# Eight-step graph diffusion, graph convolution with LSTM windows, batch-normed graph layer and edge attention in one kernel: another order of the convolution's steps, norm groups of one batch at the start of attention, and four outputs behind the gates

## The chip, the cores and the metric

One core of one Trainium2 chip runs the whole program. The metric is the device time of one execution in microseconds (us). Engines: PE (TensorE, matrix products), DVE (VectorE), ACT (ScalarE), POOL (GpSimd), SP (SyncE, which only issues DMAs here). Each engine runs its own instructions in the order in which they were written; semaphores hold it where it needs another engine's result.

## What is computed

`x` has 16 batches of 512 nodes with 128 features, `adj` is 512x512. Four graph layers follow each other, each with a residual and a layer norm behind it:

```python
def _layernorm(x, axis=-1, eps=1e-05):
    m = jnp.mean(x, axis=axis, keepdims=True)
    v = jnp.var(x, axis=axis, keepdims=True)
    return (x - m) / jnp.sqrt(v + eps)

# L0: eight Euler steps on h = x @ fc_in_w.T + b
ax = jnp.einsum('nm,bmd->bnd', adj_mx, h)
f = alph * 0.5 * (ax - h) + h @ w_eff - h + x0
h = h + dt * f
# L1: two graph convolutions, then LSTMs over windows of 1, 2, 3 and 4 nodes
h = jax.nn.relu(jnp.einsum('ts,bsh->bth', adj, x @ Wg0 + bg0))
h = jax.nn.relu(jnp.einsum('ts,bsh->bth', adj, h @ Wg1 + bg1))
for p in range(1, MAX_SKIP + 1):   # last hidden state of each window replaces a node
    ...
# L2: normalised adjacency, 128 -> 256 -> 128 with two batch norms
# L3: attention over 256 edges with 4 heads (leaky relu, softmax by source, scatter)
x = _layernorm(x + L0(x)); x = _layernorm(x + L1(x))
x = _layernorm(x + L2(x)); x = _layernorm(x + L3(x))
```

## The kernel before

The program has four phases: the operators (powers of the diffusion matrix), `phase_main`, `phase_batchnorm` and `phase_attention`. Most products are made in three passes of high and low parts (`product`, L65 to L67): a value is copied to its high part (ACT) and the low part is the difference (`low_part`, L78, on DVE or POOL).

`phase_main` takes the 16 batches in four quads q = 0 to 3. Its work is a list `order` of items, such as `("c", q, b, layer, c)`; each engine walks through the same list and does its own part of each item. So the list sets the order on every engine. While the LSTM steps of quad q run (`X` is a step's product with the input, `L` the product with the state and the gates, `C` the cell's tanh and the new state, `H` the split of the next input), the items of `stages(q + 1)` fill the space between them. The planner (`cuts`, `FILL`, `WORK`) divides them by PE work. The items that matter here:

- `s` (q, pair a, half j): the last diffusion product; DVE adds half the pair's chunks to X (L1471). `st1`: row statistics of X for the first layer norm (L570, one instruction of 128x128 per chunk). `ln1`: six small DVE operations (L1486 to L1491) and a power on POOL (L1774). `sh1`: the shift (L1507, DVE). `ap1`: the norm applied by ACT, four ACTIVATEs of 128x128 (L1305). `xs`: X split into XSh (ACT, L1281) and XSl (POOL), which the mix products read; `xs(q, 6)` and `xs(q, 7)` belong to batches 2 and 3 of the quad.
- `c` (q, b, layer): mixing over nodes, 12 products of 512 columns. In layer 1 ACT makes yh (L1311) and DVE yl. `v`: the product with the weights. After layer 0, DVE adds the bias (L1524), ACT makes relu's high part (`relu`, L1315) and DVE its low part B2l (L1534), which `c` of layer 1 waits for. The ring of PSUM banks for these items has four banks.
- `set`: transposes of weights at the start (quad 0 only). `r`, `st2`, `ln2`, `sh2`, `ap2`: residual and second norm of the quad before. In the last quad the filling is the batch-normed layer: `a` (aggregate, GHh by ACT L1375 and GHl by DVE), `w` (widen; ACT writes z_hidden, L1382, and DVE takes its statistics, L1606), `xz` (split of X).

Behind the last LSTM step the list ends with a hand-written tail of `a`, `w`, `norm2` and `applied2` for the last quad.

`phase_attention` has its own list: `z` (ACT, L2283), `T` (transpose on PE, added to X by DVE, L2355), `s3`/`v3`/`p3`/`sh3`/`ap3` (third norm: statistics, variances, power on POOL L2461, shift L2377, apply on DVE L2407 and ACT L2311), `xs` (aXH by ACT L2291, aXL by POOL), `G` (gather, PE L2202, waits for aXL), `U`, `lr`, `W` (scores, PE L2221, waits for lr of DVE). `GROUPS3` says which batches share one norm step. `busy` is a run of PE filler products (L73). `first_part` writes the begin of the list and `slot(k)` one slot per batch.

## Time and profile before

| | us |
|---|---|
| median of 3 runs | 1003.17 |
| lowest and highest | 1000.18, 1003.86 |
| the profiled execution | 1001.52 |
| its span in the trace | 999.7 |
| PE busy | 934.2 (93% of the span) |
| DVE, ACT, POOL busy | 658.8, 545.4, 312.3 |

The trace is of one execution. A line of a timeline gives the start, the duration, the engine, the source line and the operation with the tiles that it writes and reads; a bracket at its end is the idle time of that engine just before, and who ended it. A line of a table by stretches gives the busy time of each engine in that stretch and, as PEclk, the clock that was granted to PE as a share of full speed (1.00 is 2.4 GHz, 0.50 is 1.2 GHz). PE's ends are modelled and consecutive products overlap.

### The profile page before, as it was taken

The page shows a single profiled execution, that of the slowest core. Times are in us where ns is not written, and L with a number is a line of the kernel's source. Part 1 is how long each engine was busy: PE and PEld are TensorE (multiplying, and loading weights), DVE is VectorE, ACT ScalarE, POOL GpSimd, SP SyncE. Part 2 cuts the span into 40 slices and gives each one's busy share as a digit, 9 for nine tenths or more (in the row PEclk, how much of TensorE's full clock was granted, in tenths as well). Part 3 has the DMA queues.
Part 4 walks back from the last instruction along what each step waited for, and adds up shares of the span by engine and source line. Part 5 has one row for each costly group of instructions (what it writes and reads, how often), then busy time and mean ns, then how long its engine had stood idle before and what let it go on. Part 6 is the DMA issues. An engine that isn't in the chain of part 4 may idle for free. (4 is left out here: it accounts for less than half of the span.)

```text
span 999.7 us, 14585 instructions
## 1 busy us (share of the span) xinstructions
PE 934.2 (93%) x5210; PEld 803.4 (80%) x5210; DVE 658.8 (66%) x1627; ACT 545.4 (55%) x1136; POOL 312.3 (31%) x290
## 2 busy tenths in 40 slices
PE   7999997999998999998999999899989989988994
PEld 6689986899997888998889899888778864566773
DVE  7665345445646657665655775598897876788867
ACT  2042314664645565554656464557667647476667
POOL 3011222332233234223323323224333230155663
PEclk9999999999999999999999999999999999999998
DMA  8040011001010100101010010401010000000014
GB/s 226 2 83 22 20 45 64 1 22 43 1 44 1 43 22 1 43 2 43 1 43 22 1 44 1 125 1 45 20 43 22 1 1 1 1 1 1 1 43 127
DMA packets 33996, 31.64 MB, mean 32 GB/s; under 512 B 8451, under 2 KB 28035, under 8 KB 33925
## 3 DMA queue, kind: packets, MB, share of 16 engines
q1 hardware_dynamic: 32900, 30.64, 10.0%
q8 instruction: 42, 0.69, 0.3%
q14 instruction: 30, 0.24, 0.1%
q10 hardware_dynamic: 960, 0.07, 0.1%
q0 software_dynamic: 64, 0.00, 0.0%
HBM read 22.83 MB, written 7.87 MB: 31 GB/s over the span
## 5 line engine op out<-in xcount | busy, mean ns | idle before, releaser
L1344 ACT ACTIVATE gates<-psum,gbias 128x256 f32<-128x256 f32 (+2 forms) x312 | 158.9, 565 | 66.2 <-PE psum L67 61.4
L65 PE MATMUL psum<-LS,WI 128*128 128x256 f32 (+2 forms) x312 | 104.3, 334 | 9.3 <-ACT gates L1344 5.7
L67 PE MATMUL psum<-LS,WI 128*128 128x256 f32 (+2 forms) x312 | 103.0, 330 | 0.0
L66 PE MATMUL psum<-LS,WI 128*128 128x256 f32 (+2 forms) x312 | 102.9, 330 | 0.0
L78 POOL TENSOR_TENSOR LS<-A,LS 128x512 fp32r<-128x512 f32 (+2 forms) x44 | 49.0, 1113 | 170.7 <-ACT LS L1329 170.7
L78 POOL TENSOR_TENSOR LS<-Hodd,LS 128x512 fp32r<-128x512 f32 (+2 forms) x44 | 48.7, 1106 | 147.9 <-ACT LS L1329 147.9
L78 DVE TENSOR_TENSOR yl<-psum,yh 128x512 fp32r<-128x512 f32 x58 | 39.6, 688 | 65.1 <-ACT yh L1286 44.2
L78 POOL TENSOR_TENSOR XSl<-X,XSh 128x512 fp32r<-128x512 f32 x32 | 42.6, 1335 | 114.4 <-ACT XSh L1281 114.4
L1351 ACT ACTIVATE tc<-cell 128x512 f32<-128x512 f32 (+2 forms) x88 | 45.3, 514 | 54.9 <-DVE cell L1639 30.7
L65 PEld LDWEIGHTS psum<-LS,WI 128*128 128x128 f32 x312 | 59.3, 190 | 18.4 <-POOL LS L78 10.0
L65 PE MATMUL psum<-B2h,LT2h 128*128 128x256 f32 x256 | 72.7, 284 | 1.0 <-DVE X L1457 1.0
L67 PE MATMUL psum<-B2h,LT2l 128*128 128x256 f32 x256 | 72.4, 283 | 0.0
L66 PE MATMUL psum<-B2l,LT2h 128*128 128x256 f32 x256 | 72.4, 283 | 0.0
L66 PEld LDWEIGHTS psum<-LS,WI 128*128 128x128 f32 x312 | 59.4, 190 | 5.0
L67 PEld LDWEIGHTS psum<-LS,WI 128*128 128x128 f32 x312 | 59.4, 190 | 4.2
L65 PE MATMUL psum<-LS,WH 128*128 128x256 f32 (+2 forms) x192 | 60.4, 314 | 0.0
L66 PE MATMUL psum<-LS,WH 128*128 128x256 f32 (+2 forms) x192 | 60.0, 312 | 0.0
L67 PE MATMUL psum<-LS,WH 128*128 128x256 f32 (+2 forms) x192 | 60.0, 312 | 0.0
L65 PE MATMUL psum<-Eh,yh 128*128 128x384 f32 x168 | 56.6, 337 | 0.0
L67 PE MATMUL psum<-Eh,yl 128*128 128x384 f32 x168 | 56.3, 335 | 0.0
L66 PE MATMUL psum<-El,yh 128*128 128x384 f32 x168 | 56.2, 335 | 0.0
L570 DVE BATCH_NORM_STATS2 nstats<-X 128x6 f32<-128x128 f32 x256 | 54.1, 277 | 0.4
(378 smaller groups left out, 2696.7 us busy)
## 6 DMA issues: line engine op xcount, KB each, us to landing
WI<-lstm_weights SPq DMA_DIRECT2D x14, 512.0 KB, 3.5
WH<-lstm_weights SPq DMA_DIRECT2D x11, 512.0 KB, 4.6
X<-in_x SPq DMA_DIRECT2D x16, 256.0 KB
out<-X SPq DMA_DIRECT2D x16, 256.0 KB, 2.3
lstm_weights<-WI SPq DMA_DIRECT2D x4, 512.0 KB, 3.0
lstm_weights<-WH SPq DMA_DIRECT2D x3, 512.0 KB, 2.7
A<-in_adj SPq DMA_DIRECT2D x4, 256.0 KB, 4.3
z_A<-in_adj SPq DMA_DIRECT2D x1, 1024.0 KB, 5.4
```

The costliest lines, as they stand in the source:

```text
L65: pe.matmul(out, lhs[0], rhs[0], start=start, stop=False)
L66: pe.matmul(out, lhs[0], rhs[1], start=False, stop=False)
L67: return pe.matmul(out, lhs[1], rhs[0], start=False, stop=stop)
L78: return eng.tensor_tensor(out, full, high.bitcast(F32), ALU.subtract)
L570: return dve.bn_stats(self.stats[:, bass.ds(self.sh.C * n + c, 1), :], self.sh.X[:, c, bass.ds(n, 1), :])
L1344: act.activation(gates[:, gate, 0:n], sh.psum[:, gate, 0:n], ACT.Tanh if gate == G else ACT.Sigmoid, bias=gbias[:, p_ - 1, gate:gate + 1]) ...
L1351: act.activation(tcs[:, 0:n], cell[:, s % 2, 0:n], ACT.Tanh).then_inc(S["tanh_done"], 1)
```

## The change

1. `giant("s")` now has `st1(q, a, 0)` between its two halves and `first_norm` only `st1(q, a, 1)`. A `st1` item takes the chunks of one half for both batches (four instructions) where it took all chunks of one batch.
2. In `stages`, the first layer's weighing and the norm of pair 1 are interleaved anew; `applied(q, 2)` (sh1 and ap1 of batch 2) and `split(q, 6)` come ahead of `c(q, 0, 1)`; both `c` of layer 1 stand together; `applied(q, 3)` and `split(q, 7)` come behind them.
3. In quad 0 five of the weight transposes (`set`) stand at places of their own, most of them later.
4. In the last quad, `extra` (second norm of quad 2) comes ahead of the second half of the filling. In the tail, `st2(3, 3)` and `ln2` come behind `aggregated(z_ - 1)`.
5. `gates_first`: ACT and DVE take `w` items that stand directly ahead of an `L` behind it. With this list that is one output in steps 12 and 17 each and both in step 20 of the last quad, four in all.
6. Attention: batches 0 to 3 are norm groups of one, batches 4 to 15 pairs (before: 0, 1, 2, then pairs from 3, and 15). The items of `first_part` and of slots 0 and 1 are in another order; `aXL` of batch 0 is made by DVE in an item `xl`; 16 filler products in place of 24.

```diff
-            return [(kind, q, a, j) for j in (0, 1)] + ([("th", q, a)] if kind == "t" else [])
+            if kind == "t":
+                return [("t", q, a, 0), ("t", q, a, 1), ("th", q, a)]
+            return [("s", q, a, 0), ("st1", q, a, 0), ("s", q, a, 1)]
...
-            return [("st1", q, a, 0), ("st1", q, a, 1), ("ln1", q, a)]
+            return [("st1", q, a, 1), ("ln1", q, a)]
...
-                    giant("s", q, 1), weigh(q, 0, 0), first_norm(q, 1), weigh(q, 1, 0), mix(q, 0, 1), applied(q, 2),
-                    applied(q, 3), split(q, 6), mix(q, 1, 1), split(q, 7), weigh(q, 0, 1), weigh(q, 1, 1), mix(q, 2, 0),
...
+                     giant("s", q, 1), [("v", q, 0, 0), ("st1", q, 1, 1), ("relu", q, 0), ("ln1", q, 1), ("v", q, 1, 0),
+                                        ("relu", q, 1)]]
+            second = [*applied(q, 2), *split(q, 6)]
+            if q == 0:
+                sets = [[("set", n)] for n in range(NSET - SETS_LATE, NSET)]
+                return parts + [sets[0], sets[1], second, mix(q, 0, 1), mix(q, 1, 1), applied(q, 3), split(q, 7),
+                                weigh(q, 0, 1), weigh(q, 1, 1), sets[2], mix(q, 2, 0),
+                                ahead[0], mix(q, 3, 0), ahead[1], weigh(q, 2, 0), weigh(q, 3, 0), sets[3], mix(q, 2, 1),
+                                mix(q, 3, 1), weigh(q, 2, 1), sets[4], weigh(q, 3, 1)]
...
-                order += first_[:cut_] + before + first_[cut_:] + [("X", q_, k_)] + second_ + extra + [("L", q_, k_)]
+                order += first_[:cut_] + before + first_[cut_:] + [("X", q_, k_)]
+                order += (extra + second_ if q_ == NQ - 1 else second_ + extra) + [("L", q_, k_)]
...
-        order += applied2(q_, 0, 2) + [("xz", z_)] + widened(z_ - 3) + norm2(q_, 2, 4) + aggregated(z_ - 1)
+        order += applied2(q_, 0, 2) + [("xz", z_)] + widened(z_ - 3) + [("st2", q_, 2)] + aggregated(z_ - 1) + [("st2", q_, 3), ("ln2", q_, 2, 4)]
...
+        def gates_first(items):
+
+            moved, held = [], []
+            for n, item in enumerate(items):
+                upto = next((i for i in range(n, len(items)) if items[i][0] not in ("w",)), len(items))
+                if item[0] in ("w",) and upto < len(items) and items[upto][0] == "L":
+                    held.append(item)
+                    continue
+                moved.append(item)
+                if item[0] == "L":
+                    moved += held
+                    held = []
+            return moved
...
-        GROUPS3 = [(0, 1), (1, 2), (2, 3)] + [(b, min(b + 2, NB)) for b in range(3, NB, 2)]
+        GROUPS3 = [(b, b + 1) for b in range(QB)] + [(b, b + 2) for b in range(QB, NB, 2)]
...
             if k == 0:
-                items += [("s3", t - 1), ("v3", 3)]
+                items += [("sh3", 2), ("ap3", 2), ("xs", 2), ("sh3", 3), ("ap3", 3)]
+            else:
+                items += [("xs", 3)] * (k == 1) + [("sh3", i) for i in ready] + [("ap3", k + 3)] * (k + 3 < NB)
...
-                    keep_busy(pe, sh.psum[:, 7, :], GsT[:, 0, 0:P], GZ[:, 0, :, :], 24)
+                    keep_busy(pe, sh.psum[:, 7, :], GsT[:, 0, 0:P], GZ[:, 0, :, :], 16)
```

Three places show how the rows move. First DVE in quad 1, around LSTM steps 14 and 15 of quad 0. L1524 adds the bias of a layer 0 weighing, L1534 makes the low part for the mix, L570 are row statistics, L1486 to L1491 the variances, L1633 is the next LSTM step's cell. Before:

```order
L1524 TENSOR_TENSOR B<-psum,RB 128x512
L1534 SCALAR_TENSOR_TENSOR B2l<-B,B2h 128x512
L570 BN_STATS nstats<-X 128x6 x8
L1486 TENSOR_TENSOR n1work<-nstats 128x8
L1487 TENSOR_TENSOR n1work<-nstats 128x8
L1488 TENSOR_TENSOR n1work<-nstats 128x8
L1489 SCALAR_TENSOR_TENSOR n1work<-n1work 128x8
L1490 SCALAR_TENSOR_TENSOR n1work<-n1work 128x8
L1491 TENSOR_SCALAR n1work<-n1work 128x8
L1524 TENSOR_TENSOR B<-psum,RB 128x512
L1633 TENSOR_TENSOR cell<-gates 128x256
```

The same place on DVE now (L1549, L1559, L1510 to L1515 and L1658 are the same statements):

```order
L1549 TENSOR_TENSOR B<-psum,RB 128x512
L570 BN_STATS nstats<-X 128x6 x4
L1559 SCALAR_TENSOR_TENSOR B2l<-B,B2h 128x512
L1510 TENSOR_TENSOR n1work<-nstats 128x8
L1511 TENSOR_TENSOR n1work<-nstats 128x8
L1512 TENSOR_TENSOR n1work<-nstats 128x8
L1513 SCALAR_TENSOR_TENSOR n1work<-n1work 128x8
L1514 SCALAR_TENSOR_TENSOR n1work<-n1work 128x8
L1515 TENSOR_SCALAR n1work<-n1work 128x8
L1549 TENSOR_TENSOR B<-psum,RB 128x512
L1658 TENSOR_TENSOR cell<-gates 128x256
```

Four of the eight statistics went ahead of the low part, the other four stand several rows earlier, between the two additions to X.

Second ACT in quad 0, from the relu of layer 0 on (B2h is relu's high part, WH and WI are weight transposes, X with n1shift is ap1, XSh the split, yh the evacuation of a layer 1 mix). Before:

```order
L1274 ACTIVATE WH<-psum 128x512
L1315 ACTIVATE B2h<-B 128x512 x2
L1274 ACTIVATE WI<-psum 128x512
L1311 ACTIVATE yh<-psum 128x512
L1305 ACTIVATE X<-X,n1shift,n1scale 128x128 x8
L1281 ACTIVATE XSh<-X 128x512
```

Now:

```order
L1339 ACTIVATE B2h<-B 128x512 x2
L1298 ACTIVATE WH<-psum 128x512
L1329 ACTIVATE X<-X,n1shift,n1scale 128x128 x4
L1305 ACTIVATE XSh<-X 128x512
L1335 ACTIVATE yh<-psum 128x512 x2
L1329 ACTIVATE X<-X,n1shift,n1scale 128x128 x4
```

Four of the eight norm operations and a split now stand ahead of the first evacuation yh.

Third ACT at the begin of attention (X with n3shift is ap3, aXH the split, A is z, aZ and aUV evacuate G and U). Before:

```order
L2311 ACTIVATE X<-X,n3shift,n3scale 128x128 x2
L2291 ACTIVATE aXH<-X 128x512
L2283 ACTIVATE A<-O_10372,bsh,bsc 128x512
L2295 ACTIVATE aZ<-psum 128x512
L2295 ACTIVATE aUV<-psum 128x512
L2311 ACTIVATE X<-X,n3shift,n3scale 128x128 x6
L2291 ACTIVATE aXH<-X 128x512
```

Now:

```order
L2348 ACTIVATE X<-X,n3shift,n3scale 128x128 x2
L2328 ACTIVATE aXH<-X 128x512
L2348 ACTIVATE X<-X,n3shift,n3scale 128x128 x3
L2320 ACTIVATE A<-O_10380,bsh,bsc 128x512
L2332 ACTIVATE aZ<-psum 128x512
L2332 ACTIVATE aUV<-psum 128x512
L2328 ACTIVATE aXH<-X 128x512
```

The split of batch 3 stood behind the norm of batches 3 and 4 together; the norm of batch 3 now comes ahead of a z and two evacuations, and that of batch 4 behind the split.

## Rows read from the trace of the kernel before

**Rows 1.** The page's head: span, and PE's busy time, share and count.
```profile
span 999.7 us, 14585 instructions
PE 934.2 (93%) x5210; PEld 803.4 (80%) x5210; DVE 658.8 (66%) x1627; ACT 545.4 (55%) x1136; POOL 312.3 (31%) x290
```
**Rows 2.** Stretches: length, busy PE, PEld, DVE, ACT, POOL, then PEclk, DMA, GB/s.
```profile
476.50:479.90 3.40, 3.40 (x12) 2.82 (x11) 0.00 (x1) 3.37 (x8) 0.55 (x1) 0.51 0.00 0
306.00:309.40 3.40, 2.40 (x11) 2.03 (x12) 1.53 (x4) 1.87 (x6) 0.00 (x0) 1.00 0.00 0
...
732.50:735.90 3.40, 3.14 (x11) 3.08 (x12) 3.36 (x10) 2.21 (x6) 0.18 (x1) 0.51 0.00 0
...
811.00:814.40 3.40, 3.40 (x10) 2.63 (x9) 2.70 (x8) 1.08 (x2) 1.00 (x1) 0.51 0.00 0
```
**Rows 3.** Timelines in quad 1, last row quad 2: start, duration, operation, idle before.
```profile
300.72 0.47 PE L65 MATMUL psum<-ATh,B2h 128*128 128x512 f32 x1 [1.13 <-DVE B2l L1534]
307.00 0.47 PE L65 MATMUL psum<-ATh,B2h 128*128 128x512 f32 x1 [1.87 <-DVE B2l L1534]
312.26 0.36 PE L65 MATMUL psum<-LS,WI 128*128 128x256 f32 x1 [0.86 <-ACT gates L1344]
...
300.49 1.63 DVE L570 BATCH_NORM_STATS2 nstats<-X 128x6 f32<-128x128 f32 x8
...
303.01 0.68 DVE L1524 TENSOR_TENSOR B<-psum,RB 128x512 f32<-128x512 f32 x1
...
306.18 0.68 DVE L1534 SCALAR_TENSOR_TENSOR B2l<-B,B2h 128x512 fp32r<-128x512 f32 x1
...
307.56 3.19 ACT L1305 ACTIVATE X<-X,n1shift,n1scale 128x128 f32<-128x128 f32 x8 [1.53 <-DVE n1shift L1507]
...
475.00 0.47 PE L65 MATMUL psum<-ATh,B2h 128*128 128x512 f32 x1 [1.87 <-DVE B2l L1534]
```
**Rows 4.** Timelines of PE and POOL in quad 0.
```profile
127.08 0.38 PE L65 MATMUL psum<-B2h,LT2h 128*128 128x256 f32 x1 [1.00 <-DVE X L1457]
...
153.34 0.47 PE L65 MATMUL psum<-ATh,B2h 128*128 128x512 f32 x1 [2.09 <-DVE B2l L1534]
...
159.47 0.50 PE L65 MATMUL psum<-yh,Wg1h 128*128 128x512 f32 x1 [2.02 <-DVE yl L78]
...
151.29 1.64 POOL L1774 TENSOR_TENSOR n1scale<-n1work,const 128x8 f32<-128x8 f32 x1 [14.19 <-DVE n1work L1491]
```
**Rows 5.** Timeline of PE in quad 3.
```profile
638.09 0.47 PE L65 MATMUL psum<-ATh,B2h 128*128 128x512 f32 x1 [2.24 <-DVE B2l L1534]
```
**Rows 6.** Timelines of PE and DVE in the last quad's LSTM steps.
```profile
732.76 0.63 PE L65 MATMUL psum<-LS,WI 128*128 128x340 f32 x1 [2.58 <-POOL LS L78]
...
725.50 1.12 DVE L584 TENSOR_SCALAR X<-X,nscale,nshift 128x128 f32<-128x128 f32 x4
...
727.14 0.68 DVE L1637 TENSOR_TENSOR gates<-gates,cell 128x512 f32<-128x512 f32 x1
727.86 1.67 DVE L1639 TENSOR_TENSOR cell<-gates 128x512 f32<-128x512 f32 x1
```
**Rows 7.** Timelines of PE and DVE in the tail of the main phase.
```profile
809.70 0.50 PE L65 MATMUL psum<-z_GHh,z_WTh 128*128 128x512 f32 x1 [2.74 <-DVE z_GHl L78]
...
806.45 1.63 DVE L570 BATCH_NORM_STATS2 nstats<-X 128x6 f32<-128x128 f32 x8
```
**Rows 8.** Timelines of PE, ACT and POOL at the begin of attention.
```profile
870.55 6.60 PE L73 MATMUL psum<-z_GZ,z_GsT 128*128 128x512 f32 x24
...
884.73 0.50 PE L2202 MATMUL psum<-z_GZ,aXH 128*128 128x512 f32 x1 [0.74 <-POOL aXL L78]
...
891.20 0.50 PE L2202 MATMUL psum<-z_GZ,aXH 128*128 128x512 f32 x1 [1.19 <-POOL aXL L78]
...
886.86 2.42 ACT L2311 ACTIVATE X<-X,n3shift,n3scale 128x128 f32<-128x128 f32 x6 [1.85 <-DVE n3shift L2377]
...
875.90 1.31 POOL L78 TENSOR_TENSOR aXL<-X,aXH 128x512 fp32r<-128x512 f32 x1 [1.30 <-ACT aXH L2291]
```

More of the change, by code:

```diff
@@ L846, in prologue @@
             rest = rest[rest.index(giant("t", 0, 1)) + 1:]
-            for part in rest:
-                parts.append(part)
-                if part and part[0][0] in ("v", "s"):
-                    parts.append([next(late, None)])
-            parts.append(list(late))
-            return [item for item in flat(parts) if item is not None] + [("H", 0, 0)]
+            parts += rest
+            assert sum(item[0] == "set" for item in flat(parts)) == NSET
+            return flat(parts) + [("H", 0, 0)]
         WORK = {"xt": 43, "y": 68, "b": 156, "t": 272, "s": 272, "c": 68, "r": 43, "at": 43, "wt": 43, "a": 68, "w": 68}
@@ L1387, in conv_weights @@
                 act.activation(Wg1h[:, :], Wg1, ACT.Copy).then_inc(S["wg_hi"], 1)
-            for item in order:
+            for item in gates_first(order):
                 kind, at = item[0], item[1:]
@@ L1491, in variances, with first_stats @@
                 return dve.tensor_scalar(b, b, EPS, None, ALU.add)
-            def first_stats(q, a, b):
-                if b == 0:
-                    dve.wait_ge(S["ring_free"], ring["s", q, a, 1] + 1)
-                ins = norm.take_stats(dve, QB * q + 2 * a + b)
-                if b == 1:
+            def first_stats(q, a, j):
+                dve.wait_ge(S["ring_free"], ring["s", q, a, j] + 1)
+                for b in (0, 1):
+                    for c in range(2 * j, 2 * j + 2):
+                        ins = norm.row_stats(dve, QB * q + 2 * a + b, c)
+                if j == 1:
                     link(ins)
@@ L1686, in conv_constants @@
                 dve.tensor_tensor(gbias[:, :, :], bi[:, :, :], bh[:, :, :], ALU.add).then_inc(S["gbias_done"], 1)
-            for item in order:
+            for item in gates_first(order):
                 kind, at = item[0], item[1:]
@@ L2035, in slot @@
             closing = False
-            ready = [i for i, (b0, b1) in enumerate(GROUPS3) if b1 == t and k > 1] + [2] * (k == 0) + [3] * (k == 1)
-            items = [("p3", i) for i in ready if i > 2]
+            ready = [i for i, (b0, b1) in enumerate(GROUPS3) if b1 == t and b0 >= QB]
+            items = [("p3", i) for i in ready]
             if 0 <= m + 1 < NB:
@@ L2153, in group_of, with x_low @@
             return next(g for g, (b0, b1) in enumerate(groups) if b0 <= n < b1)
+        def x_low(eng, n):
+            eng.wait_ge(S["xh_done"], n + 1)
+            if n and x_low_on_dve(n) != x_low_on_dve(n - 1):
+                eng.wait_ge(S["xl_done"], n)
+            low_part(eng, by_chunk(XL[:, n % 2, :]), xb(n), by_chunk(XH[:, n % 2, :])).then_inc(S["xl_done"], 1)
         def weighted_low(eng, n):
@@ L2427, in _ @@
                     apply(n, 3, chunks3(n)[0]).then_inc(S["x3_dve"], 1)
+                elif kind == "xl" and x_low_on_dve(n):
+                    x_low(dve, n)
                 elif kind == "lr":
@@ L2476, in _ @@
                     roots(3, GROUPS3, n)
-                elif kind == "xs":
-                    pool.wait_ge(S["xh_done"], n + 1)
-                    low_part(pool, by_chunk(XL[:, n % 2, :]), xb(n), by_chunk(XH[:, n % 2, :])).then_inc(S["xl_done"], 1)
+                elif kind == "xs" and not x_low_on_dve(n):
+                    x_low(pool, n)
                 elif kind == "va":
```

26 lines of the change are left out of this document (15 added, 11 removed).

## The prediction

> **What bounds the kernel.** I read the page's head first: PE is busy for 93% of the span [rows 1]. So a microsecond counts only if it is taken from PE's products, from its idle time or from its clock. The products don't change, but for eight fillers. The next view was PE's timeline with the idle time in brackets, read through for idle times of over 0.4 us: they come to an estimated 54 us and stand nearly all where a quad's second pair is mixed, in the last quad, in the tail of the main phase and at the begin of attention [rows 3 to 8]. The mixes of layer 1 wait for `B2l` alone twelve times, an estimated 14.5 us in all. Last I looked at the granted clock: full nearly everywhere, and half in three stretches of 3.4 us, each of which follows an idle time of 1.87 to 2.74 us [rows 2, 3, 6, 7]. PE does half the work in such a stretch, so each costs 1.7 us. The sum below is made against the profiled execution, 1001.52 us (span 999.7, so 1.8 us lie around it). The median of the runs shown, 1003.17, lies 1.65 above it, which I add at the end.
>
> **Quads 1 and 2.** On DVE eight row statistics take 1.63 us, 0.20 each [rows 3]. Before, all eight and the variances (six small operations, ended at 303.0) stand between the low part of batch 0 and the addition of batch 1 (L1524) at 303.01. The mix of batch 1 waits for the low part of that chain, L1534 at 306.18, until 307.00: 1.87 us idle [rows 3]. Now four of the eight stand between the two `s` halves, where DVE would wait for PE anyway, and the other four go ahead of the first low part. The addition at 303.01 no longer has eight statistics right ahead of it but four, which are covered in part by ACT's relu; I put it at 301.7. Between it and L1534 lie 3.17 us in which an LSTM step goes through DVE and ACT; nothing of that changes, so the chain moves as a whole and the mix starts 1.3 us earlier. The first mix's wait, 1.13 at 300.72 [rows 3], stays or grows by 0.15 at most, since four statistics now lie in front of its low part. Then the gates: PE waits 0.86 at 312.26 for ACT's gates, which stand behind eight norm operations of 3.19 us [rows 3]. With four of them there (1.6 us) that wait goes: 0.85 more. Against it, the norm of batch 3 and its split stand behind the gates of the next step and cost an estimated 0.35 there. 1.3 + 0.85 − 0.35 = **1.8 each, 3.6 together**. What hides the norm and split of batch 2, which ACT now does ahead of the first `yh`, are an `L`, an `X` and an `L` of the LSTM on PE, an estimated 4.8 us; POOL's root (1.64 in quad 0 [rows 4]), the shift, four norm operations (1.6) and a split come to some 4.6. Without that cover the mixes' products would stand still; that is the rival on the slow side.
>
> **Quad 0** has no LSTM steps beside it. In the first pair half of the statistics leave the path of the wait of 1.00 at 127.08 for DVE's addition [rows 4]; half of 1.63 is 0.8, and a part of it lay hidden: **0.5**. In the second pair the mix of batch 1 waits 2.09 for its low part and the first weighing 2.02 for `yl` [rows 4]. The first of these goes to near 0.15, since the statistics are no longer in the chain. But ACT now has root (1.64 [rows 4]), shift, four norm operations and a split ahead of the first `yh`, and PE has only one mix, 2.9 us, to fill that: the first weighing waits about as long as now, 2.1. Both `yl` are then ready together, and the next weighing's short wait goes. Walked through row by row, the mix of batch 2 starts some 3.3 us earlier; of that two later waits, for the norm of batch 3, take back 0.3. **3.0**, between 1.5 and 4.0. The later transposes only fill space.
>
> **Quad 3** has the same order, but there DVE has less room: the step's hidden state comes behind four statistics more. I expect the 2.24 at 638.09 [rows 5] to grow to some 3.1, and the smaller waits behind it, 0.7 together, to vanish: **0**.
>
> **Last quad.** The norm of an earlier batch by DVE (1.12, L584) stands between `GHl` and the gates' products [rows 6]; now it comes ahead of `GHl`. The LSTM chain behind it (0.68, 1.67 and on to the split by POOL) is what PE waits 2.58 for at 732.76 [rows 6]. The whole 1.12 would leave it if DVE had been idle ahead of `GHl`; it is nearly so: **1.0**, between 0.3 and 1.7. The four outputs behind the gates save nothing where ACT's evacuation isn't late for PE, and PE's order is the same: 0, with ±0.5.
>
> **Tail.** The statistics of both batches (1.63 at 806.45) stand ahead of the last-but-one low part `GHl`, and PE waits 2.74 for it at 809.70 [rows 7]. Now four of the eight are behind it, and the variances too: the output product can start 1.65 earlier. The root on POOL is then a little late for the split that follows, 0.25: **1.4**.
>
> **Attention.** The 24 fillers take 6.60 us, from 870.55 to 877.15 [rows 8]. Sixteen end some 1.9 earlier. The first gather waits for `aXL(0)`: by POOL 1.31 us from 875.90, to 877.21 [rows 8]; by DVE, by the size of L1534 (0.68 [rows 3]), it is ready near 875.8. So 1.4 is possible, but gathers 1 and 2 depend on norm steps that come no earlier: new waits of some 1.3 and 1.0 behind gather 0 eat most of this. What does come earlier is the split of batch 3. ACT's norm of batches 3 and 4 together, 2.42 from 886.86, lies ahead of it, and the gather waits until 891.20 [rows 8]; alone and earlier, it is ready some 2.8 sooner. The 1.19 there goes, the 0.74 at 884.73 [rows 8] stays, and scores and leaky relus behind take some back: **2.0**, between 0 and 3.5.
>
> One rule speaks against it. In the last quad L1639 with its two inputs in SBUF takes 1.67 beside a split on POOL, and L1637, the same size, 0.68 without [rows 6]. The Trainium skill says for this (SBUF — State Buffer, "Who interferes with whom") that a DVE instruction that reads two inputs from SBUF and a GpSimd one lock each other out of the port; the trace agrees with the 1.67 against 0.68. By that rule `xl` on DVE could stand behind a root on POOL of 1.0 us or more, and the attention term would be 1.0 in place of 2.0.
>
> **Clock.** The three half-speed stretches begin behind idle times of 1.87 (475.00), 2.58 (732.76) and 2.74 (809.70), all of which shrink [rows 3, 6, 7]. But quad 1 has 1.13 and 1.87 as well and keeps the full clock [rows 2, 3], so an idle time makes a drop possible, not sure; and new ones of over 2 us come (quad 0, quad 3). I take one drop fewer, **1.7**. The Trainium skill (TensorE: Matmul & The Clock Gate, "What's actually happening") holds that the window in which the activity is looked at runs freely of the kernel; by that no single drop can be foretold, and the term could be anything from −1.7 to 5.1. The two quads with the same idle times and different clocks agree.
>
> **Sum.** 0.5 + 3.0 + 3.6 + 0 + 1.0 + 1.4 + 2.0 = 11.5, and 1.7 for the clock: 13.2. 1001.52 − 13.2 = 988.3, and 1.65 to the median: **990.0**. Its own range is 986 to 994, from the ends of quad 0, the last quad and attention.
>
> **Rivals.** Differences under 0.5% (5 us) are about what a measurement of this kernel can't tell from none; so faster means below 998.2 and slower above 1008.2.
>
> *Later waits take it back.* PE starts a mix earlier, but the LSTM chain (gates on ACT, two passes through DVE, a split on POOL) sets the pace of a quad, and PE meets it one item further on. For it: the 0.86 for the gates [rows 3] shows the chain just behind PE. Against it: PE is nearly full between the places named. If quads 1 and 2 keep 1.0 of 3.6, quad 0 keeps 2.0, attention 0.5 and the clock nothing, 6.4 are left of 13.2: 996.8.
>
> *All three clock drops go.* 3.4 more than the forecast: 986.6; with the upper ends of attention and quad 0 983.
>
> *Nothing measurable.* Quad 3's larger idle time, and a drop behind it, against gains of 3 us: 1002.
>
> *Slower: ACT blocked by the norm of batch 2.* In ACT's queue `yh` of both mixes and the next gates now stand behind an operation that waits for `n1shift`. It decides when the shift comes later than PE's cover: 4.6 against 4.8 is a small margin. Where it is missed by 2 us in each of three quads, PE stands for 2.1 and its clock halves behind it for 1.7, in each; and in quad 0 once more 1.7: 11.4 + 1.7 = 13.1 lost, against 3.0 in quad 0 and 4.9 of the tail, the last quad, attention and the first pair kept: 5.2 slower, 1008.4. Against it: before, ACT's norm had waited only 1.53 for the shift [rows 3], and the shift comes earlier now.
>
> **Chances.** Forecast 0.52, later waits 0.23, all drops gone 0.12, nothing 0.08, slower 0.05. The range 983 to 999 leaves out the last two and little of the others. Below 998.2 lie the forecast, the third case and most of the second: faster 0.83, same 0.12, slower 0.05.
>
> **What would show it.** In the profile after: PE's waits for `B2l` in quads 1 and 2 should be near 1.2 and 0.6 in place of 1.13 and 1.87, and that for the gates should be gone. Quad 0 should have one wait of some 2 us for `yl` and none above 0.5 for `B2l`. The tail's 2.74 should be near 1.1, the last quad's 2.58 near 1.6. In attention the gather of batch 3 should not wait, and two small waits should stand behind the first gather. The forecast is wrong if PE waits over 2 us for `yl` or gates in quads 1 to 3, if over two stretches at half clock are left, or if the idle time lost at these places reappears in the LSTM steps between them.

## The result, and the profile after

The changed kernel took 996.02 us (median of 4 runs, 994.48 to 996.82) beside 1003.12 for the kernel before; the ratio is 0.9936, with a 95% interval of 0.9919 to 0.9953. In a later series of runs it took 995.86 beside 1001.0, ratio 0.9941 (0.9919 to 0.9963). One of the eight executions of that series took 1053.4 us at a mean granted clock of 0.843, where the others had 0.981 to 0.988, and is left out of the ratio. So the change is worth 5 to 7 us. The forecast was 13.2 us. The sign held and so did the wide range of 983 to 999; the forecast's own range, 986 to 994, did not, and the size was about twice too large.

Its page's head, and PE's idle times at the places that the forecast named:

```profile
span 994.9 us, 14572 instructions
PE 933.1 (94%) x5202; PEld 801.6 (81%) x5202; DVE 664.6 (67%) x1628; ACT 546.2 (55%) x1136; POOL 311.3 (31%) x289
```

PE's timeline after, quad 0 (two rows), quad 1 (two), quad 3, last quad (two), tail (two), attention (two):

```profile
127.77 0.38 PE L65 MATMUL psum<-B2h,LT2h 128*128 128x256 f32 x1 [1.00 <-DVE X L1481]
...
155.89 0.50 PE L65 MATMUL psum<-yh,Wg1h 128*128 128x512 f32 x1 [1.80 <-DVE yl L78]
...
299.55 0.47 PE L65 MATMUL psum<-ATh,B2h 128*128 128x512 f32 x1 [1.25 <-DVE B2l L1559]
...
317.59 0.47 PE L65 MATMUL psum<-ATh,XSh 128*128 128x512 f32 x1 [0.55 <-POOL XSl L78]
...
633.65 0.47 PE L65 MATMUL psum<-ATh,B2h 128*128 128x512 f32 x1 [3.14 <-DVE B2l L1559]
...
727.60 0.41 PE L65 MATMUL psum<-LS,WI 128*128 128x340 f32 x1 [1.54 <-POOL LS L78]
...
732.71 0.39 PE L65 MATMUL psum<-LS,WI 128*128 128x340 f32 x1 [2.78 <-ACT gates L1368]
...
804.39 0.50 PE L65 MATMUL psum<-z_GHh,z_WTh 128*128 128x512 f32 x1 [1.00 <-DVE z_GHl L78]
...
806.76 0.50 PE L65 MATMUL psum<-z_AhTh,z_XZh 128*128 128x512 f32 x1 [0.70 <-DVE z_st L1631]
...
884.45 0.39 PE L2258 MATMUL psum<-lr,wide 128*16 128x256 f32 x1 [1.64 <-DVE lr L2422]
...
908.52 0.39 PE L2258 MATMUL psum<-lr,wide 128*16 128x256 f32 x1 [2.06 <-DVE lr L2422]
```

In quad 1 the wait of 1.87 and the one of 0.86 for the gates [rows 3] are gone and no row answers to them; in quad 0 the 2.09 is gone, the 2.02 is 1.80 and the 1.00 is 1.00 still [rows 4]. The tail's 2.74 [rows 7] is 1.00 and 0.70. Quad 3's 2.24 [rows 5] is 3.14, as foreseen. The last quad's 2.58 [rows 6] is 1.54, but one step later stands a wait of 2.78 that was shorter before:

```profile
737.88 0.39 PE L65 MATMUL psum<-LS,WI 128*128 128x340 f32 x1 [1.39 <-ACT gates L1344]
```

The clock, as stretches of 3.4 us in the columns of [rows 2], with quad 2's place, at full clock, last:

```profile
156.20:159.60 3.40, 3.40 (x12) 2.72 (x11) 2.53 (x5) 1.92 (x5) 1.48 (x1) 0.54 0.00 0
633.60:637.00 3.40, 3.35 (x9) 2.66 (x10) 2.01 (x8) 1.19 (x3) 1.64 (x1) 0.61 0.77 185
732.60:736.00 3.40, 3.29 (x13) 3.32 (x14) 3.40 (x9) 2.34 (x5) 1.17 (x1) 0.61 0.02 5
810.00:813.40 3.40, 3.40 (x17) 2.81 (x16) 2.10 (x8) 1.83 (x4) 1.37 (x1) 1.00 0.00 0
910.30:913.70 3.40, 3.40 (x11) 2.64 (x11) 3.33 (x11) 0.49 (x1) 1.14 (x2) 0.58 0.00 0
470.00:476.00 6.00, 5.80 (x37) 5.15 (x37) 2.88 (x7) 4.83 (x11) 1.30 (x1) 1.00 0.00 0
```

The half-speed stretches of quad 2 and the tail are gone, and that of the last quad is left. New ones stand in quad 0, quad 3 and attention, each behind one of the waits above (1.80, 3.14, 2.06). Two of the prediction's own signs of being wrong are met: over two stretches at half clock are left, and PE waits over 2 us for gates, in the last quad.

To see where the time went I took sections between events that every trace has: starts of ACT's tanh of the cell (88 in the main phase), of a `GHh`, of the first `z`, of a leaky relu (lr) and of a split of the weighted values (`va`); the last row ends with the last norm on ACT, 4.5 us before the span's end. Lengths in us:

| section | before | after | forecast's gain | gain |
|---|---|---|---|---|
| begin to the first split | 60.17 | 60.74 | – | −0.57 |
| quad 0, to the first tanh | 129.38 | 127.52 | 3.5 | 1.86 |
| quad 1, tanh 15 to 23 | 59.23 | 57.44 | 1.8 | 1.79 |
| quad 2, tanh 23 to 45 | 168.49 | 166.22 | 1.8 | 2.27 |
| quad 3, tanh 45 to 67 | 165.89 | 167.14 | 0 | −1.25 |
| last quad, tanh 67 to 81 | 77.12 | 77.59 | 1.0 | −0.47 |
| last quad, tanh 81 to 88 | 28.10 | 27.86 | 0 | 0.24 |
| tail, to the 13th `GHh` | 22.41 | 20.37 | 1.4 | 2.04 |
| attention, first `z` to lr 5 | 40.44 | 40.04 | 2.0 (all of attention) | 0.40 |
| lr 5 to the fifth split of `va` | 30.85 | 33.34 | | −2.49 |
| from there to the end | 56.62 | 55.63 | | 0.99 |

The other sections are equal. The sum is 4.8, as the spans say. The forecast's 1.7 for the clock is in no row of its own. The first row is not the change's: over the traces of the kernels with the changed order it runs from 58.51 to 60.74, and a stretch at half clock of 3.4 or 6.8 us lies around its end in every trace, before and after. Two readings are open from this: whether quad 0, quad 3 and the last quad lost their gain by the clock, and what attention lost 2.49 us on.

### The profile page after: what moved, and what is told of

It is laid out like the page before. It is cut to its first block and busy times, and to the rows that moved or that the text cites. A ratio compares the mean times of both kernels' runs of the same rounds, so it can differ in the third digit from the quotient of the medians.

```text
span 994.9 us, 14572 instructions
## 1 busy us (share of the span) xinstructions
PE 933.1 (94%) x5202; PEld 801.6 (81%) x5202; DVE 664.6 (67%) x1628; ACT 546.2 (55%) x1136; POOL 311.3 (31%) x289
## 5 line engine op out<-in xcount | busy, mean ns | idle before, releaser
L65 PEld LDWEIGHTS psum<-LS,WI 128*128 128x128 f32 x312 | 59.2, 190 | 17.4 <-POOL LS L78 10.2
L570 DVE BATCH_NORM_STATS2 nstats<-X 128x6 f32<-128x128 f32 x256 | 54.9, 278 | 0.5
```

The lines of the kernel that those rows point to most:

```text
L65: pe.matmul(out, lhs[0], rhs[0], start=start, stop=False)
L570: return dve.bn_stats(self.stats[:, bass.ds(self.sh.C * n + c, 1), :], self.sh.X[:, c, bass.ds(n, 1), :])
```

## The experiments

Eleven variants and the changed kernel itself once more, in five rounds each, in four series. The kernel before ran beside them, with medians of 1001.0 (first four), 1002.25 (next four), 1001.95 (next three) and 1002.64 (last), so ratios compare best across series. The ratio of the changed kernel is 0.994.

### The changed kernel again

> The changed kernel once more, unchanged, beside the three below. Both theories: 996 us, ratio to the kernel before 0.993. What it is for is the clock. Theory A (a drop to half clock can follow any idle time of PE of over some 1.5 us, and which ones it follows changes from execution to execution): the granted clock falls in other places than in the first profile, where it fell behind the idle times of 1.80 us in quad 0, 3.14 in quad 3, 1.54 in the last quad and 2.06 in attention. Theory B (each of these four always loses its clock, since its idle time is long enough): the same four places again.

995.86 us. The half clock stood behind the 3.15 of quad 3, the 2.78 of the last quad and the 2.06 of attention again, but not behind the 1.80 of quad 0. (What was expected names the 1.54 of the last quad; in both traces the half clock there begins at the end of the 2.78, one step later.)

```profile
152.50:159.50 7.00, 5.20 (x25) 4.01 (x24) 3.92 (x7) 5.67 (x13) 2.58 (x2) 1.00 0.15 62
631.90:635.30 3.40, 3.37 (x8) 2.75 (x9) 2.00 (x8) 1.20 (x3) 1.64 (x1) 0.51 0.76 183
730.90:734.30 3.40, 3.36 (x12) 3.39 (x13) 3.40 (x8) 2.34 (x5) 1.09 (x1) 0.51 0.02 5
```

So neither theory holds alone. Over all traces of kernels with the same wait: 1.80 in quad 0 was followed by half clock in 4 of 9, 2.06 in attention in 7 of 9, 3.14 in quad 3 in 6 of 7, 2.78 in the last quad in 9 of 9. Behind the two long ones the clock fell in 15 of 16 cases, behind the two shorter in 11 of 18. Each of these waits stands in one place of the program, so the count does not separate the length of the wait from the place. Quad 3's place with a wait of 2.24 lost its clock in 2 of 3 traces.

### Fillers in the waits of quads 0 and 3

```diff
+                        if q == 3 and b == 0:
+                            keep_busy(pe, bank(n), AT[0][:, 0, 0:P], AT[0][:, 0, :], 12)
                         pe.wait_ge(S["h1l_done"], QB * q + b + 1)
...
+                if layer == 1 and q == 0 and b == 0:
+                    begin(n)
+                    keep_busy(pe, bank(n), AT[0][:, 0, 0:P], AT[0][:, 0, :], 7)
                 pe.wait_ge(S["ring_free"], ring["c", q, b, layer] + 1)
```

> The changed kernel with filler products in two of PE's idle times: 7 (1.6 us) ahead of the first weighing of layer 1 in quad 0, 12 (2.8 us) ahead of the first mix of layer 1 in quad 3, each into the bank that the next product overwrites. Nothing waits for them. If the idle time brings the drop to half clock behind it: both stretches at half clock (near 156.4 and 634) are at full clock, and since each costs up to 1.7 us the kernel is 2 to 3.4 us faster, 992.6 to 994. If the drops have nothing to do with the idle time, or what follows waits anyway: the same 996, or up to 0.5 more, since fillers can end a little late.

992.34 us, ratio 0.9912: 3.5 less than the changed kernel beside it (991.25 to 993.56 against 994.02 to 997.0), just beyond the 2 to 3.4 that was expected. Both stretches are at full clock (the second is 6.8 us long and holds quad 3's place):

```profile
152.50:159.50 7.00, 6.76 (x32) 5.26 (x32) 4.98 (x8) 4.58 (x10) 2.60 (x2) 1.00 0.05 22
...
629.50:636.30 6.80, 6.51 (x33) 5.32 (x32) 3.07 (x11) 3.86 (x9) 2.51 (x2) 1.00 0.60 140
```

Quad 0's section is 125.57 us (before: 129.38), quad 3's 165.50 (before 165.89, changed 167.14). Products that compute nothing, placed where PE waits, made the kernel faster. What they give in these two sections is the clock alone: the kernel with batch 4 alone (below) has neither fillers nor half clock there in its trace, and its sections are 125.59 and 165.55. In all four kernels with fillers at both places neither lost its clock in its trace, where without them quad 0's fell in 4 of 9 and quad 3's in 6 of 7. At 1.6 us for each drop this makes an estimated 2.1 us on average; where the rest of the 3.5 comes from is not shown.

### Relu first in quad 3

```diff
+            if q == NQ - 1:
+                parts[-1] = [("v", q, 0, 0), ("relu", q, 0), ("st1", q, 1, 1), ("ln1", q, 1), ("v", q, 1, 0), ("relu", q, 1)]
```

> The changed kernel, but in quad 3 alone the four last row statistics of the second pair stand behind the addition and relu of the first weighing, not between them, so that DVE makes the low part for the first mix ahead of them. If these four (0.87 us) on DVE are what made the wait of 2.24 us grow to 3.14: it is 2.3 again, quad 3 gains 0.9 us, and up to 2.6 if the half-clock stretch behind it goes too: 993.4 to 995.1. Rival: the wait ends with the same LSTM step in either case, and the second mix's low part is now behind the four, so that the gain comes back as a wait of 0.9 ahead of the second mix: 996.

994.42 us, ratio 0.9928. The wait is 2.24 again and quad 3's section 166.22, 0.92 less than changed; the half clock behind it stayed. No wait came ahead of the second mix. The four statistics were the whole growth of the wait. Most of the 0.92, though, is the clock: with fillers and so at full clock this order gives 165.29 (the combined kernel below) against 165.50.

### Attention as before

Only attention's list, groups, `xl` and 24 fillers are those of before.

> The changed kernel with the attention phase as it was before (norm groups, order of the items, low part of batch 0 on POOL, 24 fillers); the main phase is the changed one. My forecast gave the new attention 2.0 us of gain: by it this run is 2.0 us slower than the changed kernel, 998.0. The trace of the changed kernel says otherwise: attention starts 5.9 us earlier than before and ends 4.4 earlier, so it lost 1.5; by it this run is 1.5 us faster, 994.5. A third reading is that the loss is one half-clock stretch that came by chance: then the two are within 1 us.

994.54 us, ratio 0.9935. That is 1.3 less than the changed kernel by the medians, within what the two spreads allow. The section from lr 5 to the fifth split is 31.37 (changed 33.34), the rest 57.42 (changed 55.63); the trace of this run has 6.8 us at half clock in that rest, from 962.7, and the changed kernel's has none there. The new attention is no gain; how large its loss is this pair doesn't settle.

### Batch 4 as a group of its own

```diff
-        GROUPS3 = [(b, b + 1) for b in range(QB)] + [(b, b + 2) for b in range(QB, NB, 2)]
+        GROUPS3 = [(b, b + 1) for b in range(QB + 1)] + [(b, min(b + 2, NB)) for b in range(QB + 1, NB, 2)]
...
-            ready = [i for i, (b0, b1) in enumerate(GROUPS3) if b1 == t and b0 >= QB]
+            ready = [i for i, (b0, b1) in enumerate(GROUPS3) if b1 == t and b0 > QB] + [QB] * (k == 1)
```

> The changed kernel with batch 4 in a third-norm group of its own as well, then pairs from 5 on, as before. In the changed kernel the variances of a pair (five small DVE operations, 0.75 us) stand in the attention slot in which DVE also does the first softmax (two scans and a sum), right ahead of the leaky relu that PE waits 2.06 us for at 908.52; the kernel before had them one slot earlier and waited 1.29. If that is where the forecast's 2.0 us of attention went: this wait is near 1.3 again, the half-clock stretch behind it may go, and the stretch from the fifth leaky relu to the fifth weighted value takes 1.5 to 2.5 us less: 993.5 to 994.4. Rival: DVE is full in this stretch whatever the order, and the same time is waited for one slot earlier or later: 995.9.

993.98 us, ratio 0.9913 (0.9891 to 0.9936), 0.0028 under the changed kernel's 0.9941, or 2.8 us; the two intervals overlap a little. The trace is of the fastest of its six executions (989.48 us), which kept its clock in quads 0 and 3 and in this part of attention. DVE's timeline ahead of the leaky relu, first of the changed kernel, then of this one:

```profile
906.50 0.85 DVE L570 BATCH_NORM_STATS2 nstats<-X 128x6 f32<-128x128 f32 x4
907.38 0.17 DVE L2402 TENSOR_TENSOR n3work<-nstats 128x8 f32<-128x8 f32 x1
...
907.96 0.17 DVE L2406 SCALAR_TENSOR_TENSOR n3work<-n3work 128x8 f32<-128x8 f32 x1
908.04 0.42 DVE L2422 SCALAR_TENSOR_TENSOR lr<-aUV 128x256 f32<-128x256 f32 x1
```

```profile
900.44 0.87 DVE L570 BATCH_NORM_STATS2 nstats<-X 128x6 f32<-128x128 f32 x4
901.23 0.41 DVE L2422 SCALAR_TENSOR_TENSOR lr<-aUV 128x256 f32<-128x256 f32 x1
```

and PE's row behind it:

```profile
901.69 0.39 PE L2258 MATMUL psum<-lr,wide 128*16 128x256 f32 x1 [1.29 <-DVE lr L2422]
```

The five variances (0.7 us with their gaps) are out of the slot that also holds the scans of the softmax, and the wait is 1.29 in place of 2.06. The section from lr 5 to the fifth split is 30.84, 2.5 less than changed and equal to before (30.85). Against a trace of the changed groups without half clock there (33.19) it is 2.35. The rival, that DVE is full in this stretch in any order, falls; 0.7 of the gain is lost again behind it. The variances are not all that the shift of the groups moved. DVE's first scan of the softmax stood beside a split on POOL in the changed kernel and stands beside none here:

```profile
902.25 1.79 DVE L2426 TENSOR_TENSOR_SCAN s<-pf,sco 16x256 f32<-16x256 f32 x1
```

```profile
896.19 0.68 DVE L2426 TENSOR_TENSOR_SCAN s<-pf,sco 16x256 f32<-16x256 f32 x1
```

How much each of the two costs was not separated.

### The old slot order in the last quad

The diff of the change for `extra` and `second_` is taken back.

> The changed kernel with the old place of the second norm's application in the last quad: behind the second half of the filling, right ahead of the gates. My forecast gave its new place 1.0 us (PE's wait of 2.58 became 1.54, which came true), so by it this run is 1.0 slower, 996.9. The trace says that the wait one step later grew from 1.39 to 2.78 and that a half-clock stretch, which fell into that wait before, now falls behind it: the 14 steps around take 77.6 us in the changed kernel and took 77.1. By it this run is 0.5 us faster, 995.4, with the waits 2.58 and 1.39 again.

996.92 us, ratio 0.9944 (0.9927 to 0.9962), not to be told from the changed kernel's. The waits are

```profile
727.55 0.41 PE L65 MATMUL psum<-LS,WI 128*128 128x340 f32 x1 [2.59 <-POOL LS L78]
...
732.68 0.62 PE L65 MATMUL psum<-LS,WI 128*128 128x340 f32 x1 [1.75 <-ACT gates L1368]
```

so they are near those of before, as the trace said. But the 14 steps took 79.88 us in this trace, since half clock lasted for 10 us, from shortly behind the 2.59 on:

```profile
728.60:738.60 10.00, 8.25 (x26) 7.17 (x26) 9.86 (x23) 5.26 (x12) 3.77 (x3) 0.50 0.01 2
```

In the trace of the kernel before [rows 2] it lasted for 3.4. The medians can't tell 1.0 slower from 0.5 faster. The trace can, if the 14 steps are taken apart at the tanhs:

| us between tanhs of the last quad | 73 to 75 | 75 to 77 | 77 to 80 | half clock in it from |
|---|---|---|---|---|
| before | 13.03 | 10.56 | 14.84 | 732.4, for 3.4 |
| changed | 11.97 | 10.56 | 16.35 | 733.3, for 3.4 |
| old slot order | 13.03 | 11.39 | 16.76 | 728.5, for 10.2 |
| fillers here too (`fill_last`, below) | 11.99 | 10.57 | 14.82 | none |

The first column is the order's: 13.03 in the two traces with the old order, 11.96 to 11.99 in all twelve with the new. So the new place gains 1.06, as forecast, and my expectation of 0.5 faster was wrong. The third column is the clock's: 16.35 where it falls behind the wait for the gates, 14.82 where it doesn't.

In the kernel before the clock fell inside the wait of 2.58, 0.4 us before its end:

```profile
729.00:732.40 3.40, 1.18 (x6) 0.63 (x4) 2.02 (x4) 2.08 (x4) 0.72 (x1) 1.00 0.00 0
732.40:735.80 3.40, 3.04 (x10) 3.05 (x11) 3.36 (x10) 2.21 (x6) 0.28 (x1) 0.51 0.00 0
```

PE's slow products then ran into the wait for the gates, which was 1.39 for it instead of 2.78, and the steps took no longer than at full clock (14.84 against 14.82).

The gain of 1.06 came only in part in the way that the forecast gave. DVE in the changed kernel, and the splits on POOL beside it, first the changed kernel's, then that of the kernel before:

```profile
719.65 1.86 DVE L584 TENSOR_SCALAR X<-X,nscale,nshift 128x128 f32<-128x128 f32 x4
...
723.35 0.69 DVE L1664 TENSOR_TENSOR cell<-gates 128x512 f32<-128x512 f32 x1
...
724.74 1.01 DVE L1671 TENSOR_TENSOR Hodd<-gates,tc 128x512 f32<-128x512 f32 x1
...
723.47 1.74 POOL L78 TENSOR_TENSOR z_XZl<-X,z_XZh 128x512 fp32r<-128x512 f32 x1 [2.29 <-ACT z_XZh L1385]
```

```profile
727.57 1.40 POOL L78 TENSOR_TENSOR z_XZl<-X,z_XZh 128x512 fp32r<-128x512 f32 x1 [2.31 <-ACT z_XZh L1361]
```

From tanh 73 on (722.13 before, 718.03 changed) DVE reaches the cell's addition 0.41 earlier, not 1.12, because the norm now takes 1.86. The addition takes 0.69 in place of 1.67 [rows 6], since it now starts ahead of POOL's split and not behind its start: 0.98. The new state behind it takes 1.01 in place of 0.69: 0.32 lost. 0.41 + 0.98 − 0.32 is 1.07.

### All eight statistics together

```diff
-            return [("s", q, a, 0), ("st1", q, a, 0), ("s", q, a, 1)]
+            return [("s", q, a, 0), ("s", q, a, 1)]
...
-            return [("st1", q, a, 1), ("ln1", q, a)]
+            return [("st1", q, a, 0), ("st1", q, a, 1), ("ln1", q, a)]
```

and in `stages` relu of batch 0, both `st1`, `ln1` and the next weighing in this order.

> The changed kernel with all eight row statistics of a pair together again behind the first weighing and its relu, as before; everything else in the new order. The forecast's term for quads 1 and 2: 1.3 us each of the 1.8 come from the split, the rest (0.85 less 0.35) from the norm of batch 3 standing later. So quads 1 and 2 are 1.3 slower each, quad 0 some 1.9 slower, quad 3 0.9 faster, 3.6 in all: 999.5. Rival: what helps is that the norm and the split of batch 2 go first, and the wait of 1.87 would be gone even with the statistics together: within 1 us of 995.9.

999.73 us, ratio 0.998 (0.9965 to 0.9995), where 999.5 was expected; by the ratios 3.9 more than the changed kernel, where 3.6 was expected. The wait of quad 1 is back:

```profile
304.14 0.47 PE L65 MATMUL psum<-ATh,B2h 128*128 128x512 f32 x1 [1.86 <-DVE B2l L1559]
```

Quad 2's section is 167.75, 1.53 more than changed; quad 1's 60.56, 3.1 more, with a half-clock stretch behind the 1.86 in it, which makes the difference to quad 2; quad 3's 166.23, 0.9 less. Quad 0's section is 127.25 without a drop behind its 1.80, 1.7 more than the 125.59 of a trace free of half clock there, where 1.9 was expected. The split of the statistics carries over half of the change's gain.

### The norm late again in quads 1 to 3

```diff
-            return parts + [second, mix(q, 0, 1), mix(q, 1, 1), applied(q, 3), split(q, 7), weigh(q, 0, 1)
+            return parts + [mix(q, 0, 1), applied(q, 2), applied(q, 3), split(q, 6), mix(q, 1, 1), split(q, 7), weigh(q, 0, 1)
```

> The changed kernel with, in quads 1 to 3, the norms of batches 2 and 3 and the split of batch 2 behind the first mix of layer 1, and the second split behind the second mix, as before. By the forecast this brings back the wait of 0.86 for the gates in quads 1 and 2 and takes away the 0.55 for XSl that the changed kernel shows there: 0.5 us slower in each of the two, nothing in quad 3: 996.9. If the new place were what made the slow rival possible (ACT stuck behind n1shift), this run would be faster than 995.9; the trace of the changed kernel shows no such wait, so I don't expect that.

997.87 us, ratio 0.9954 (0.9939 to 0.997), against 996.9 expected. By the ratios that is 1.3 more than the changed kernel, and the intervals overlap; the sections tell more. The wait for the gates comes back larger than before:

```profile
307.74 0.36 PE L65 MATMUL psum<-LS,WI 128*128 128x256 f32 x1 [1.53 <-ACT gates L1368]
```

Quad 1's section is 0.94 and quad 2's 0.93 longer than changed, and quad 3's 0.6, where nothing was expected. The forecast had put this part at 0.5 in each of quads 1 and 2.

### Without the outputs behind the gates

The engines walk `order` itself in place of `gates_first(order)`.

> The changed kernel without the reordering of outputs behind the gates on ACT and DVE (four outputs in steps 12, 17 and 20 of the last quad). The forecast put it at nothing, within 0.5 us: 995.4 to 996.4. Rival: steps 14 to 21 of the last quad take 27.86 us in the changed kernel and took 28.10 before, and this part of the change is what stands there: the run is 0.2 to 0.3 us slower in these steps, which only the trace can show.

995.79 us, ratio 0.9936. Steps 14 to 21 take 28.10 as before, and the tail up to the 13th `GHh` 20.04 in place of 20.37. The 0.25 that this part gains is given back behind it. It can't be told from nothing, as forecast.

### Fillers in the last quad, and the parts together

```diff
+                if (q, k) == (NQ - 1, 9):
+                    begin(ring["w", 3, 1])
+                    keep_busy(pe, bank(ring["w", 3, 1]), WI[:, slot, 0, 0, :], WI[:, slot, 0, :, :], 10)
                 pe.wait_ge(S["xs_done"], NS * q + k + 1)
```

> The kernel of the run with fillers, and 10 more (2.3 us) in the last quad, ahead of the input products of step 9, where PE waits 2.78 us for the gates; they go into a bank that a later output product overwrites. In all nine traces of kernels with the new order there, a stretch at half clock stands behind this wait, and the 14 steps around take 77.6 us each time. If the wait causes it: those steps take 76.0 to 76.4 here, 1.2 to 1.6 us less, and the kernel is that much faster than the one with fillers in two places only: about 991. Rival: the LSTM chain through ACT, DVE and POOL sets the pace of these steps, PE's slow products are waited for anyway by nobody: 77.6 again and 992.3.

992.15 us, ratio 0.9905. I had the place wrong: these ten stand in the wait of 1.54, and the one for the gates (2.31 in this trace) stayed unfilled. The clock is full behind it all the same, and the 14 steps take 76.07, 1.5 less:

```profile
729.20:732.60 3.40, 3.37 (x20) 3.27 (x21) 3.40 (x8) 2.35 (x6) 1.07 (x1) 1.00 0.00 0
```

The median gained 0.2 only.

> The changed kernel with what the runs so far point to: relu first in quad 3, batch 4 as a norm group of its own in attention, and fillers in the three idle times (7 in quad 0, 8 in quad 3, 10 in the last quad). If the gains add up: 3.5 for the two filled places, 2.0 for the norm groups, 0.9 for the relu, 1.4 for the last quad, 7.8 in all: 988. If the fillers cost what the shorter wait in quad 3 gains, or the last quad is bound by its LSTM chain: 989 to 990.5.

990.30 us, ratio 0.9889 (0.9873 to 0.9905), in the second of the two expected ranges: the gains do not add up in full. Here the same wait of 2.30 was followed by half clock, and the 14 steps took 77.62:

```profile
728.17 0.39 PE L65 MATMUL psum<-LS,WI 128*128 128x340 f32 x1 [2.30 <-ACT gates L1378]
...
728.20:731.60 3.40, 3.40 (x14) 3.29 (x15) 3.38 (x8) 2.32 (x5) 1.04 (x1) 0.65 0.00 0
```

The last run has 5 fillers ahead of step 9 and 9 ahead of step 10, where the gates are waited for:

> The combined kernel with the last quad's fillers at two places. The ten of the runs before stood ahead of the input products of step 9, that is in the wait of 1.54 us for LS, and not in the one of 2.78 us for the gates, which belongs to step 10. Now 5 (1.2 us) stand ahead of step 9 and 9 (2.1 us) ahead of step 10. With ten ahead of step 9 alone the half-clock stretch was gone in one trace (76.07 us for the 14 steps) and there in the other (77.62). If it is the longer wait that the drop follows: the 14 steps take 76.1 and the kernel 1.5 us less than the combined one, 988.8. If the drop comes in spite of a filled wait, or the fillers end too late: 77.6 and 990.3.

989.01 us, ratio 0.9868 (0.9841 to 0.9895), the lowest median of all, though its interval overlaps the combined kernel's. PE's wait is 0.71, the 14 steps take 76.09, and no stretch there is below full clock:

```profile
727.40:730.80 3.40, 2.81 (x17) 2.71 (x18) 3.40 (x8) 2.32 (x7) 1.66 (x2) 1.00 0.00 0
730.80:734.20 3.40, 3.40 (x22) 3.27 (x22) 3.33 (x9) 2.52 (x6) 1.15 (x1) 1.00 0.00 0
```

One trace with full clock in the last quad does not show that the fillers brought it, since `fill_last` kept its clock behind an unfilled wait of 2.31. This version beats both kernels: 13.6 us under the kernel before in the same series, and some 7 under the changed one by the ratios.

## Why the prediction was right and wrong

**Quads 1 and 2: right.** 1.79 where 1.8 was forecast. The parts were mis-sized against each other: the split of the statistics gives 1.5 (1.3), the place of the norms behind the mixes 0.9 (0.85 less 0.35), and the two are not independent, since they don't simply add up to 1.79. The new 0.55 for `XSl` is the 0.35 that I took off.

**Quad 0: the second pair right, the first wrong, and the clock took half.** The term of 0.5 was nothing: the first pair's wait for DVE's addition is 1.00 at 127.77 as it was 1.00 at 127.08 [rows 4], and it stands 67.03 us behind the first split where it stood 66.91. Why the statistics had not lengthened it, no run asks. From that wait to the first tanh it was 62.47 before and is 58.9 in the traces without half clock behind the 1.80: 3.6 gained against 3.0. In the changed kernel's trace it is 60.49, so the drop took 1.6 of it. (The section's 125.57 against 129.38 gives 3.8, but 0.2 of this is the half clock at its begin.) The shift did hold up ACT and PE behind it here, as forecast: ACT waits 1.54 for `n1shift` at 152.26, makes norm, split and `yh` behind it, and PE waits 1.80 for `yl`.

**Quad 3: right on the order, wrong on what follows.** Free of half clock the section is 165.55 (trace of the kernel with batch 4 alone), 0.3 less than before, although the wait is 3.15 there too. The wait of 3.14 was foreseen, but in 6 of 7 traces the clock fell behind it, which costs 1.6 (167.14 against 165.55).

**Last quad: the size right, partly by luck, and the clock took more than that.** The 1.06 between tanhs 73 and 75 is the forecast 1.0. The step that failed is "The whole 1.12 would leave it if DVE had been idle ahead of `GHl`; it is nearly so": 0.41 left it, and the rest came from an addition on DVE that no longer stands beside a split on POOL. I had that row (1.67, [rows 6]) and used it for attention only. The wait of 2.78 took nothing of the gain by itself, but half clock behind it costs 1.5 (16.35 against 14.82), where the drop before had cost nothing.

**Tail: right.** 2.74 became 1.00 and 0.70, a gain of 1.04 in waits where 1.4 was forecast; the section gained 2.04, so the vanished half clock gave an estimated 1.0, by difference, and not 1.7.

**Attention: wrong, 2.0 forecast, 1.1 lost.** The split of batch 3 did come early and its gather did not wait, as forecast. The scores wait for `lr` instead (1.64 at 884.45), and of the lead 0.4 is left by lr 5. The larger part I had not looked at: groups of one for batches 0 to 3 shift all later pairs by one slot, so that a pair's variances meet the first softmax on DVE, and its first scan a split on POOL. The shift costs 2.35 us between lr 5 and the fifth split, and the half clock there 0.15 more; 0.7 comes back behind it (56.26 in the combined kernel, which has batch 4 alone, and 55.63 with the changed groups, both without half clock there). I had read the order only at attention's begin.

**Clock: the step "one drop fewer, 1.7" is what failed most.** It failed twice. First the count: I saw three half-speed stretches before; sections of 3.4 us over the whole span show two more in attention (near 869 and 971). From quad 0 to the last microseconds of attention there are five in each of the two traces, not one fewer. Second the price. I took half of 3.4 us for each. Of those before, that of the last quad cost nothing, since the wait for the gates behind it absorbed it all. That of quad 2 cost an estimated 0.5 (quad 2 gained 2.27 where quad 1, which had no drop, gained 1.79): behind the drop PE has no idle time up to 484, where quad 1 has the 0.86 for the gates [rows 3]. The tail's cost some 1.0, that near 869 nothing (40.43 to lr 5, as in the run with the attention of before, which had no half clock there), that near 971 0.4 at most. Those of the changed kernel cost 1.6 in quad 0, 1.6 in quad 3, 1.5 in the last quad and nothing near 863 (40.04 to lr 5, and 40.09 in the second trace, which had none there). The one behind 2.06 in attention cost 0.2 (33.34 against 33.19 in the trace with relu first, which has the same waits and no drop); that DVE is the slower engine there would explain it, but no run tests it. So the change traded cheap drops, some 1.5 to 1.9 in all, for dear ones of 4.9. The term is an estimated −3.2 in place of 1.7, and with attention's 3.1 that is nearly all of the 8.4 us that are missing from 13.2.

By the rule that I weighed (the Trainium skill, TensorE: Matmul & The Clock Gate, "What's actually happening": the window runs freely of the kernel) no single drop can be foretold. The runs agree in part: the same wait of 1.80 brought one in 4 of 9 traces. But the chance is not the same everywhere: 15 of 16 at the waits of 2.78 and 3.14, and none of 8 at the waits of 1.80 and 3.14 when they were filled. So "can't be foretold" was the wrong use of it: the two long waits should have been charged with a drop each.

**The rivals.** "Later waits take it back" with 996.8 named the time nearly to the microsecond, but for a different mechanism: quads 1 and 2 kept all of their 3.6, and quad 0 and the last quad kept what the order gave until the clock took it. The number is luck. The slow side did not occur: ACT waits for `n1shift` eight times, 11.7 us in all, but only in quad 0 does PE wait behind it; in quads 1 to 3 its cover held. Taking the norm back out of the way there (`norm_late`) made these sections longer. (The upper ends that the prediction names for "all three drops go" give 984.1, not 983.)

## What to carry to other kernels

Count PE's idle times by length, not only by sum: one as long as the 2.8 and 3.1 us here is charged with the wait and with the half clock behind it, and the drop's price is what the next wait doesn't absorb: 0, 0.5 and 1.6 us here. Where such a wait can't be ordered away, products into a bank that is overwritten anyway can keep the clock; here 19 of them in two waits were worth 3.5 us. The third place, worth 1.5 in a trace that kept its clock, is not shown to need them. And when groups are resized at the begin of a loop, follow the parity of the later groups to the slot with the heaviest work on the second engine.

## What the runs showed of the hardware

A small DVE operation with two inputs in SBUF (128x8) takes 0.17 us, and took 1.26 beside a split on POOL, ending with it. In the changed kernel's attention, DVE and then POOL:

```profile
886.07 1.26 DVE L2402 TENSOR_TENSOR n3work<-nstats 128x8 f32<-128x8 f32 x1
```

```profile
886.00 1.30 POOL L78 TENSOR_TENSOR aXL<-X,aXH 128x512 fp32r<-128x512 f32 x1 [3.11 <-ACT aXH L2328]
```

The Trainium skill (SBUF — State Buffer, "Who interferes with whom") has this as a lock on the port that blocks the loser, and the trace agrees: 1.26 against 0.17. The case for which I had weighed the rule did not come: `aXL` of batch 0 on DVE took 0.69 us at 869.23 and stood for nothing, though a root (the norm's power) on POOL ran until 869.40. Longer roots did no harm either: an addition on DVE with two such inputs of 512 columns took its usual 0.69 us at 563.39, wholly within a root of 3.28 us that began at 562.22. What blocked was the split with its 512 columns, not the root with its 4 to 16.

Half clock came behind waits of very different length, not every time in the same place, and once stayed for 10 us (the old slot order), though PE was busy there but for one wait of 1.75.
